# Expert choice in an audio tower: experts computed on gathered chosen tokens, their results added through products with token marks

## The reference, cut to what matters

```python
k = min(max(int(l * C / e), 1), l)                 # 187
S = jax.nn.softmax(x @ Wg, axis=-1)
G, I = jax.lax.top_k(jnp.swapaxes(S, 1, 2), k)
ex = jnp.take_along_axis(x[:, None], I[..., None], axis=2)
hmid = gelu(einsum('bekh,ehf->bekf', ex, W1) + b1)
out = einsum('bekf,efh->bekh', hmid, W2) + b2
new_x = zeros_like(x).at[arange(b)[:, None, None], I].add(G[..., None] * out)
...
h = h + _L0_ffn_ref(_layernorm(h), ...)
```

## Time and profile before

| | us |
|---|---|
| median of 3 runs | 2936.68 (2932.05 to 2938.7) |
| the profiled execution | 2933.99 |
| its span, first to last instruction | 2932.2 |
| TensorE busy in the span | 2627.6 |
| VectorE busy | 2230.6 |
| ScalarE busy | 1926.7 |
| GpSimd busy | 1188.3 |

### The profile page before, as it was taken

The page is one execution under the profiler, slowest core; times in us unless marked ns, Lnnn a source line. Parts: engine busy times, 40 slices in busy tenths (PEclk is TensorE's granted clock), DMA queues, the critical chain, the costliest instruction groups (busy, mean ns, idle before and its releaser), DMA issues. The chain is left out here.

```text
span 2932.2 us, 55307 instructions
## 1 busy us (share of the span) xinstructions
PE 2627.6 (90%) x17000; PEld 2050.1 (70%) x17000; DVE 2230.6 (76%) x3615; ACT 1926.7 (66%) x3292; POOL 1188.3 (41%) x1160
## 2 busy tenths in 40 slices
PE   8979799999999997589999999788856997999993
PEld 7969454444444445489999999688845885888882
DVE  4545689999999984769999998577766664777875
ACT  3336277777777786378888887344445885777772
POOL 0034012323232324345555555333234776466664
PEclk9989699999999998589999999899988998999997
DMA  3109433333333320622222333500002111577748
GB/s 81 36 27 371 94 57 57 56 56 56 56 56 56 56 39 1 201 75 89 85 87 84 88 85 79 197 1 0 0 1 87 50 47 64 176 250 237 251 156 251
DMA packets 148619, 278.24 MB, mean 95 GB/s; under 512 B 27836, under 2 KB 80805, under 8 KB 141576
## 3 DMA queue, kind: packets, MB, share of 16 engines
q1 hardware_dynamic: 134920, 251.89, 31.4%
q0 software_dynamic: 13568, 24.75, 2.5%
HBM read 190.89 MB, written 87.11 MB: 95 GB/s over the span
## 5 line engine op out<-in xcount | busy, mean ns | idle before, releaser
L1049 ACT ACTIVATE probs<-score 128x748 f32<-128x748 f32 (+1 forms) x768 | 568.4, 794 | 116.4 <-PE score L874 115.0
L978 DVE TENSOR_REDUCE part_max<-to_dve 128x1 f32<-128x512 f32 (+1 forms) x768 | 480.2, 684 | 82.8 <-PE to_dve L855 82.2
L2726 DVE TENSOR_TENSOR m_hid_lo<-m_hid,m_hid_hi 128x512 fp32r<-128x512 f32 x408 | 289.2, 710 | 158.2 <-ACT m_hid_hi L2699 158.2
L1522 DVE TENSOR_TENSOR f_hid_lo_c<-f_hid_c,f_hid_hi_c 128x748 fp32r<-128x748 f32 x256 | 350.4, 1378 | 42.1 <-ACT f_hid_hi_c L1505 38.8
L855 PE MATMUL to_dve<-k_stack,q_stack 48*128 48x512 f32 (+3 forms) x1536 | 351.6, 367 | 20.2 <-DMA k_stack<-k_parts 19.3
L1418 POOL TENSOR_TENSOR f_acc_c<-f_acc_c,f_gate_c 128x748 f32<-128x748 f32 x112 | 252.9, 2258 | 259.5 <-DVE f_gate_c L1538 259.2
L874 PE MATMUL score<-q_stack,k_stack 49*128 49x374 f32 (+1 forms) x1536 | 317.5, 389 | 3.1 <-ACT probs L1049 1.0
L874 PEld LDWEIGHTS score<-q_stack,k_stack 49*128 49x128 f32 (+1 forms) x1536 | 162.0, 181 | 225.0 <-ACT probs L1049 199.7
L1500 ACT ACTIVATE f_hid_c<-f_up_c,c_b 128x374 f32<-128x374 f32 x512 | 268.5, 571 | 76.1 <-DVE f_hid_lo_c L1522 52.0
L911 PE MATMUL o_sum<-probs,v_sb 128*17 128x374 f32 (+1 forms) x3072 | 315.6, 483 | 0.1
L2622 POOL DMA_INDIRECT e_sums<-m_gated,m_row_in x216 | 213.0, 986 | 162.0 <-DVE m_gated L2744 108.6
(11 more groups left out here) (431 smaller groups left out, 6496.9 us busy)
## 6 DMA issues: line engine op xcount, KB each, us to landing
m_weights<-e_records SPq DMA_DIRECT2D x54, 1028.0 KB, 7.0
f_gate_c<-c_gates SPq DMA_DIRECT2D x128, 374.0 KB, 3.4
q_stack<-q_parts SPq DMA_DIRECT2D x192, 93.5 KB, 3.1
k_stack<-k_parts SPq DMA_DIRECT2D x192, 93.5 KB, 4.3
e_slots<-blank SPq DMA_DIRECT2D x54, 260.0 KB, 3.8
m_row_in<-e_slots SPq DMA_DIRECT2D x54, 260.0 KB, 2.9
m_weights<-e_sums SPq DMA_DIRECT2D x16, 640.0 KB
e_records<-l_parts SPq DMA_DIRECT2D x16, 512.0 KB, 3.6
```

Source lines behind the costliest of these rows:

```text
L978: dve.tensor_reduce(part_max[0:ROWS[c], k, j, c, 0:1], ring[i % RING][0:ROWS[c], :], AX.X, ALU.max).then_inc(used, 1)
L1049: act.activation(probs[0:n, s % 2, m, 2 * j:2 * j + 2, :], score[tile][0:n, :, 0:HALF], ACT.Exp).then_inc(tile_used, 1)
L1522: dve.tensor_tensor(hid_lo[:, k % RING, :], hid[:, k % 2, :], hid_hi[:, k % RING, :].bitcast(F32), ALU.subtract).then_inc(lo_done, 1)
L2726: dve.tensor_tensor(hid_lo[:, f % RING, :], hid[:, f % RING, :], hid_hi[:, f % RING, :].bitcast(F32), ALU.subtract).then_inc(lo_done, 1)
```

## The change

Steps 2 to 4 of the layer change; `mixture`, the last layer, uses `router_logits` too, but as before (`keep`).

- `router_logits` gets four slots for the normalised rows instead of two, and SyncE stores each batch's rows in memory (`c_rows`, records of 128 features and 8 probabilities).
- `choose` takes the place of `route`. ScalarE stores the probabilities into the records, 16 transfers, before its part in `later_weights`. VectorE runs the same 24 rounds, replaces each chosen token's value by a key (748 minus the token's number), and runs 24 searches and 23 replacements again, which list the 187 keys of a pair in falling order in 192 slots, so the tokens by rising number. TensorE turns the lists, and VectorE makes of them `keys_at` and the row numbers `ids`.
- `chosen_ffn` takes the place of `gated_ffn`. The work is cut into 64 units of one batch and two experts, 2 x 192 slots in three tiles of 128. GpSimd gathers the three tiles of records with indirect transfers, five units deep. They are turned, rounded and split, and the products have 192 moving columns. ScalarE adds the bias to the result, TensorE turns it back to tokens on partitions, ScalarE multiplies with the gate and rounds (`gate_rows`), and VectorE makes the remainder. VectorE also writes marks: per slot 748 columns that are 1 at the slot's token and 0 elsewhere. TensorE multiplies the marks (stationary) with rounded part and remainder side by side (256 moving columns), which adds the four units of a batch up in PSUM. VectorE adds both halves to h. Nothing loops: all 64 units are written out.

The core of the diff; "..." marks what is left out.

```diff
+        R_RING = 4
+        def await_ring(eng, b):
+            if keep is None and b >= R_RING:
+                eng.wait_ge(turned, b - R_RING + 1)
+                eng.wait_ge(saved[b % R_RING], 16 * (b // R_RING))
-        rows = sb("r_rows", [P, 2, TILES, P]) if keep is None else None
+        rows = sb("r_rows", [P, R_RING, TILES, P]) if keep is None else None
...
+                        sp.dma_start(save[b * TILES * P:(b + 1) * TILES * P, 0:P].rearrange("(c p) d -> p c d", p=P),
+                                     rows_of(b)).then_inc(saved[b % R_RING], 16)
...
-                for dst in (work, cols):
-                    then(dve.tensor_copy(dst[:, 0:512], turn[:, 0, :]))
-                    then(dve.tensor_copy(dst[:, 512:T], turn[:, 1, 0:T - 512]))
+                then(dve.tensor_copy(work[:, 0:512], turn[:, 0, :]))
+                then(dve.tensor_copy(work[:, 512:T], turn[:, 1, 0:T - 512]))
...
+                then(dve.scalar_tensor_tensor(out=work[:, :], in0=work[:, :], scalar=0.0, in1=ramp[:, :],
+                                              op0=ALU.is_lt, op1=ALU.mult))
+                for r in range(SLOTS_E // 8):
+                    some = key[:, 8 * r:8 * r + 8]
+                    then(dve.max(some, work[:, :]))
+                    if r < SLOTS_E // 8 - 1:
+                        then(dve.match_replace(work[:, :], some, work[:, :], -1.0))
+                then(dve.tensor_copy(key[:, SLOTS_E:WHOLE], key[:, 0:WHOLE - SLOTS_E]))
+                dve.sem_inc(found, 1)
+                dve.wait_ge(placed, 1)
...
+                act.wait_ge(copied, 1)
+                for b in range(B):
+                    act.dma_start(rows[b * TILES * P:(b + 1) * TILES * P, P:C_RECORD].rearrange("(c p) e -> p c e", p=P),
+                                  probs[:, :, b, :]).then_inc(kept, 16)
                 later.scalar(act)
+                act.wait_ge(kept, 16 * B)
...
+            @block.gpsimd
+                for n in range(UNITS_C):
+                    if n >= RING:
+                        pool.wait_ge(gated_n, n - RING + 1)
+                    for j in range(UNIT_TILES):
+                        at = n * UNIT_TILES + j
+                        pool.indirect_dma_start(out=row_in[:, n % RING, j, :], out_offset=None, in_=rows,
+                                                in_offset=bass.IndirectOffsetOnAxis(ap=ids[:, at:at + 1], axis=0)
+                                                ).then_inc(gathered[n % RING], 16)
...
+                def turn_back(n):
+                    pe.wait_ge(kept, 2 * n + 2)
+                    if n:
+                        pe.wait_ge(gated_n, n)
+                    for j in range(UNIT_TILES):
+                        last = pe.transpose(back[:, j, :], made[:, n % 2, j * P:(j + 1) * P], g.ident[:, :])
+                    last.then_inc(turned_back, 1)
+                def combine(n, tiles):
+                    b, i = divmod(n, PER_BATCH)
+                    pe.wait_ge(gated_n, n + 1)
+                    pe.wait_ge(marked, UNIT_TILES * (n + 1))
+                    for c in tiles:
+                        if i == 0 and b and c % 2 == 0:
+                            pe.wait_ge(added, BANKS * (b - 1) + c // 2 + 1)
+                        for j in range(UNIT_TILES):
+                            last = pe.matmul(sums[c // 2][0:ROWS[c], c % 2, :, :], marks[:, n % 2, j, c * P:c * P + ROWS[c]],
+                                             gated[:, n % 2, j, :, :], ...)
+                for k in range(-1, UNITS_C + 2):
+                    if valid(k):
+                        widen(k)
+                    if valid(k - 1):
+                        narrow(k - 1)
+                    if valid(k - 2):
+                        combine(k - 2, range(0, TILES // 2))
+                    if valid(k + 1):
+                        turn_rows(k + 1)
+                    if valid(k - 2):
+                        combine(k - 2, range(TILES // 2, TILES))
+                    if valid(k - 1):
+                        turn_back(k - 1)
...
+                def gate_rows(n):
+                    act.wait_ge(turned_back, n + 1)
+                    if n >= 2:
+                        act.wait_ge(combined, n - 1)
+                    for part in gate_parts(n):
+                        at, tile, e = part
+                        act.activation(gated[at, n % 2, tile, 0, :], back[at, tile, :], ACT.Identity, bias=zero[at, :],
+                                       scale=gate_of(n, part)).then_inc(gate_hi, 1)
...
+                def gate_rows(n):
+                    dve.wait_ge(gate_hi, GATES * (n + 1))
+                    for part in gate_parts(n):
+                        at, tile, e = part
+                        last = dve.scalar_tensor_tensor(out=gated[at, n % 2, tile, 1, :], in0=back[at, tile, :],
+                                                        scalar=gate_of(n, part), in1=gated[at, n % 2, tile, 0, :].bitcast(F32),
+                                                        op0=ALU.mult, op1=ALU.subtract)
+                    last.then_inc(gated_n, 1)
+                def mark(n, j):
+                    dve.tensor_scalar(marks[:, n % 2, j, :], ramp[:, :], keys_at[:, b, i, j:j + 1], None, ALU.is_equal
+                                      ).then_inc(marked, 1)
+                for k in range(-1, UNITS_C + 2):
+                    ... gate_rows(k - 2); at a batch's end give_back; mark(k - 1, 0); split_hid(k, 0); mark(k - 1, 1);
+                    ... split_hid(k, 1); mark(k - 1, 2); split_x(k + 1); at a batch's end measure
```

More of the change, by code:

```diff
@@ L1157, in norm @@
                 def norm(b):
[L1158 to L1159 removed]
+                    await_ring(dve, b)
                     for c in range(OWN):
@@ L1184, in _, with choose @@
                                           ALU.add)
-def route(nc, g, logits, gates, k_tokens, k_experts, tag, later):
+def choose(nc, g, logits, rows, ramp, keys_at, ids, k_tokens, tag, later):
     N = B * TILES
+    WHOLE = 2 * P
     with ExitStack() as ctx:
@@ new lines, in chosen_ffn, with experts_of, gate_parts, gate_of @@
+        gathered = [sem(f"f_gathered{k}") for k in range(RING)]
+        GATES = 4
+        def experts_of(n):
+            return [2 * (n % PER_BATCH) + e for e in range(2)]
+        def gate_parts(n):
+            one, two = experts_of(n)
+            return [(slice(0, P), 0, one), (slice(0, H), 1, one), (slice(H, P), 1, two), (slice(0, P), 2, two)]
+        def gate_of(n, part):
+            at, tile, e = part
+            return row_in[at, n % RING, tile, P + e:P + e + 1]
+        def valid(n):
+            return 0 <= n < UNITS_C
```

474 lines of the change are left out of this document (204 added, 270 removed).

## The result

The changed kernel takes 2847.05 us (median of 4 runs, 2844.66 to 2847.57) beside 2935.99 us of the kernel before in the same comparison: ratio 0.9697, 95% interval 0.968 to 0.9713, so 88.9 us less. Predicted were 2837 us in a range of 2792 to 2885. The profiled execution took 2844.66 us with a span of 2842.9 us.

What follows compares the result with a forecast made beforehand. TensorE was taken to bound the old expert stage, a dependence loop the new one. Stage -584.9 + 452.5 and later start +33.3 give -99.1 on 2934.0: 2834.9, said as 2837 us for the median; range 2792 to 2885.

Steps and rivals of the forecast that it cites:

- The 2% added for waits: Expert stage: allowance on the summed 437.5 us for waits in the loop, giving 446 us.
- What bounds the kernel, pace of products: TensorE set the old expert stage's pace; products cut from 374 to 192 columns fall from 0.170 to 0.112 us.
- The loop: Expert stage, per unit: gates, remainders, mark products and transposes back through one PSUM tile, with hand-overs, take 6.11 us.
- Marks: VectorE in the expert stage: each mark of 748 columns takes 0.55 us, or 0.95 at the two-tensor slope.
- Rival (b): Marks cost the two-tensor slope, VectorE sets 7.3 us per unit: 2868 us in all, chance 0.14.
- The stage: Expert stage with its first gathers and preparation takes 452.5 us instead of 584.9.
- The 6.5 us: Start of the expert stage: first gathers, transposes, cast and subtraction, counted from block start.
- the 9.8: Expert stage: two first units before the loop closes, 4.2 + 5.6 us.
- The choice: VectorE's longer choice of tokens outlasts the preparation of later weights, so the expert stage starts 33.3 us later.
- Rival (c): Later weights end late behind ScalarE's 16 stores of probabilities, up to 26 us: 2863 us, chance 0.08.
- Rival (d): Expert stage: GpSimd's gathers (2.95 us per unit) and VectorE's marks and subtractions exclude each other: 2947 us, chance 0.05.
- Rival (a): Gates cost as little as plain copies, TensorE sets 5.6 us per unit: 2795 us, chance 0.14.

Runs made afterwards that it cites:

- e2: Changed kernel with one plain copy in place of ScalarE's four gate operations per unit: 2841.71 us, ratio 0.9554 to the kernel before.
- e3: Changed kernel with the three transposes back placed ahead of the second nine mark products on TensorE, order only: 2846.4 us, ratio 0.9573 to the kernel before.
- e7: Changed kernel plus 28 products into an unused tile on TensorE ahead of the expert stage: 2883.75 us, ratio 0.9706, beside 0.9711 of c2.
- e1: Changed kernel without the 24 searches and 23 replacements that list chosen tokens, one copy of ramp values instead: 2862.19 us, ratio 0.9632 to the kernel before.
- e5: Changed kernel with indirect gathers for the first five units only, later units on stale rows: 2881.89 us, ratio 0.9691, beside 0.9702 of c1.
- e10: Changed kernel with the remainder of the turned rows ahead of the third mark on VectorE, order only: 2886.32 us, ratio 0.9713, beside 0.9711 of c2.
- c1: The changed kernel again, unaltered, run in the second group of experiments: 2884.5 us, ratio 0.9702 to the kernel before.
- c2: The changed kernel again, unaltered, run in the third group of experiments: 2884.8 us, ratio 0.9711 to the kernel before.
- e4: Changed kernel with the additions into h ahead of the gate remainders on VectorE, order only: 2863.46 us, ratio 0.9632 to the kernel before.
- e6: Changed kernel with the order changes of e3, e4 and e10 together, no work removed: 2831.45 us, ratio 0.9525 to the kernel before.
- e8: e6 with positions looked up in each round instead of the second searches and replacements, lists unsorted: 2804.54 us, ratio 0.9438 to the kernel before.
- e9: e8 with three gate operations instead of four, VectorE first copying two halves of the gate column into one: 2819.05 us, ratio 0.9488 to the kernel before.

## Why the prediction was right, step by step

The mechanism held: no full engine, a loop through the single tile `f_back`, and a choice that sticks out behind the later weights. That the sum came within 10 us of the measured time owes something to luck. Between the first and the last gate remainder the terms alone give 63 x 6.11 + 33 = 417.9 us, and the trace has 428.6. The 2% added for waits, 8 us, stand for no such waits, since steady units keep to 6.27 or 6.28 us. They happened to cover a loop mis-sized by 0.16 us a unit (10 us) and two slow batch ends (some 2 us), less 4 us by which batch ends were priced too high.

- **What bounds the kernel, pace of products.** Right. Products of 192 columns start 0.111 us apart (in the unit after the one shown at 1496.04, 1496.15 and 1496.27), predicted 0.112. The Trainium skill ("TensorE: Matmul & The Clock Gate", LDWEIGHTS) gives columns / 1.2, 107 ns for 128 weight columns, and the trace agrees with it, not with the 82 ns of the other rule.
- **The loop.** Right in mechanism and nearly in size: 6.27 us a unit for 6.11. Gates were 1.80 (predicted 1.83 with the hand-over), remainders 1.39 for 1.27, TensorE's part 3.08 for 3.01. e2 and e3 show that it is the loop that decides: shortening one or the other of its links, once without taking any work away, gave 44 and 38 us. The largest error of the sum was here: 0.12 us of the 0.16 lie in the remainders, four in 1.34 us where the row of two in 0.61 gave 1.22. A batch's end costs 1.69 + 0.26 = 1.95, predicted 2.2.
- **Marks.** 0.60 us alone and 0.70 in the median beside gathers, predicted 0.55 with 0.95 as the other end; the low end was the right choice. Rival (b) was out by this row alone.
- **The stage.** 459.6 us for 452.5. The 63 steps between first and last remainder took 428.6, by the sum (63 x 6.11 + 33) x 1.02 = 426. The rest of the 7 us is at the ends: 21.7 us to the first remainder for 18.1 (6.5 + 9.8 + 1.8), and 9.3 us behind the last one for about 8, with the 18 last products in 4.21 us, mostly at half clock. At the start two terms are mis-sized. The 6.5 us are 8.2 until the first widening product (lines below): the third gather is issued 3.5 us after the block's start and not 1.96, because the first is issued 0.7 us late and takes 1.22 us and the others follow 0.3 us apart. The other 2 us are in the 9.8, "laid out by the same durations": those are of a TensorE at full clock, and here products are 0.21 us apart until 1303.4, behind a TensorE that was busy for 7.3 of the 50 us from 1240 to 1290. That the clock makes these 2 us is argued from the pace and not isolated. e7 adds that a few products ahead of the stage don't bring the clock up earlier.

```profile
1289.55 0.95 POOL L1383 DMA_INDIRECT f_row_in_c<-c_rows,c_ids  x1 [0.30 <-issue]
...
1294.25 0.53 PE L1405 MATMUL f_up_c<-f_x_hi_c,c_w_hi 128*128 128x192 f32 x1 [1.22 <-DVE f_x_lo_c L1517]
```

- **The choice.** 34.8 us later for 33.3. The listing was 47.2 us as predicted and the tail 3.0 for 2.8. The copy saved (1.1 us) was eaten ahead of it: the first operation of the choice's block starts at 1175.51 instead of 1174.16. Of these 1.35 us, 0.65 are a later end of VectorE's part in the router and 0.7 a longer pause between the blocks, so "nothing either way, within 1 us" for the router was a little short. Two new casts of ramps (0.55 and 0.26 us, not in the sum) cost nothing, since VectorE still waits 1.12 us behind them for the turned probabilities. e1 shows what the prediction read from the earlier trace rows, that the cover of the later weights is gone: 24 of the 47 us can be had back, then these weights hold the block.
- **Rival (c)** was out: 0.57 us to issue a store (0.48 in the earlier trace rows), landings of 2.2 us overlapping the next issues, weights done at 1259.87, 10.6 us behind their old end (8 were predicted) and 24 ahead of the choice's.
- **Rival (d).** A slowing exists, its size does not: e5 takes the gathers away and finds 0.1 us a mark in the median, 0.2 at most, not 2.95 us a unit. It is off the path in steady units and on it at batch ends, some 5 us in all. The Trainium skill ("SBUF — State Buffer", SBUF: two separate sides) makes the port an exclusive lock for a whole instruction; the rows show a mark longer by at most 0.2 us beside a gather of 0.94, so the trace agrees that there is contention and not that the one fully blocks the other.
- **Rival (a)**, 5.6 us a unit, was the right size for a kernel whose gates are plain copies: in e2 the three units between batch ends take 5.62 us on average. In the changed kernel a gate with a scale per partition cost what the dearer row said (0.44).

## What to carry to other kernels

When a change makes every engine less than full, cost the stage as a loop of dependences and not by the busiest engine: name the buffer with a single copy, write down its links with the durations of the nearest rows, and add the hand-overs. Then try orders before work: three swaps of lines, none of which removed an instruction, gave 53 us here, and the one that left the loop alone did nothing by itself (e10). A large wait in the list of waits is no evidence by itself (e10), an unchanged total can hide a gain and a loss (e5), and a longer sequence placed behind a covered one costs only what sticks out (e1).

## What the runs showed of the hardware beyond what was expected

**The clock falls behind a short wait.** In some batch ends of the changed kernel TensorE's granted clock is at 0.5 right after its wait for the additions. In c1 (timeline of TensorE, then by stretch, columns as in the earlier trace rows):

```profile
1368.00 2.15 PE L1437 MATMUL f_sums_c<-f_gated_c,f_marks_c 128*128 128x256 f32 x9 [1.54 <-DVE h L1549]
1369.95 0.84 PE L1394 MATMUL f_turn_c<-ident,f_row_in_c 128*128 128x128 f32 x3
...
1364.00:1368.00 4.00, 2.46 (x23) 2.32 (x22) 2.93 (x10) 3.61 (x11) 1.08 (x2) 1.00 0.08 19
1368.00:1372.00 4.00, 4.00 (x21) 4.00 (x22) 4.00 (x10) 0.48 (x1) 1.76 (x2) 0.57 0.21 52
```

Nine products take 2.15 us there instead of 1.28, and the unit 9.41 us instead of 7.96. This happened at 2 of 15 batch ends in the first profile, 3 in e1, 4 in c1, 2 in c2, 2 in e7, 7 in e5 and 5 in e10; the wait was 1.5 to 2.1 us where it was looked at (first profile, c1, c2, e5, e10), and at none in e2, e3, e4, e6, e8 and e9, where TensorE's longest wait from 1400 to 1600 us was 0.6 to 1.4. One batch end outside that stretch, the first of e6, waited 2.1 us and kept its clock. That it goes with the length of the wait is what these runs show, as a tendency; why one wait of 1.54 us is followed by a slow clock and the next is not, they don't. The prediction's premise, that a stretch as full as the 34.3 of 40 us of the earlier trace rows holds 1.00, was true from 1420 to 1630 and not of the whole stage (0.97).

**A single stall of ScalarE.** In the traces of all twelve experiments ScalarE stands still once in the stage's second unit, 4.0 to 4.2 us in seven of them, 2.8 to 3.5 in four and 1.1 in e3 (behind another gap of 3.4), and no semaphore of the kernel ends that wait; in the first profile of the changed kernel it does not occur. No transfer of program instructions begins in any of these waits, which speaks against late loading of instructions. What it is stays open. It differs by up to 3 us between kernels, so no verdict here rests on less than that.
